# A recommendation tower on one Trainium2 core: a fourth product chunk split in high and low, and the fp32 chunks summed first

## The chip, the core and the metric

The program runs on one core of one Trainium2 chip. The core has five engines with an instruction queue each: PE (TensorE, matrix products), DVE (VectorE), ACT (ScalarE), POOL (GpSimd) and SP (which here only starts transfers). They run side by side and wait for one another through semaphores. The metric is the device time of one execution in microseconds. Three runs of the kernel before gave 1343.85, 1344.63 and 1345.17 us, so its median is 1344.63 us.

## The reference

For each of 1024 samples, 39 embeddings of 16 numbers are looked up. Then comes a "compressed interaction network" of three layers, and then a small dense network:

```
x0 = embeddings                     # [b, 39, 16]
xk = x0
for W in (f0, f1, f2):              # 39*39 x 128, then 128*39 x 128 twice
    z   = einsum('bfd,bgd->bfgd', x0, xk).reshape(b, f*g, d)
    cur = einsum('bpd,pm->bmd', z, W)
    outs.append(cur); xk = cur
result = concat(outs).sum(-1)       # [b, 384]
h = relu([result, dense_ctx] @ W_top1 + b_top1)
h = relu(h @ W_top2 + b_top2)
y = h @ W_top3
```

Layer 1 multiplies pairs of the 39 embeddings. Its products are the operand that this change is about.

## The kernel before

The 1024 samples are 8 batches of 128 samples. A batch is 4 groups, a group is 512 columns (32 samples by 16 numbers), and a group is 4 tiles of 128 columns. So there are 32 groups and 128 tiles; the loop counter `u` counts the 16 tiles of a batch, and `tile` is `u % 4`.

Layer 1 is computed one group ahead. It uses the symmetry of the pairs, which leaves seven chunks of up to 117 product rows. For each group and chunk, DVE forms a 117x512 product (`multiply`, L765, seven per group, at the tiles and banks of `PRODUCTS`), and PE sums the seven into one bank of PSUM (`cin1`, L462). A chunk is summed in one of two ways. Either it goes in as plain fp32, which on PE is one call and two instructions in the trace. Or it is split: ACT rounds the product to a shorter format (`split_high`, L644), POOL subtracts that from the product (`split_low`, L231), and PE makes three short passes (high by high, low weights by high, high weights by low). `SPLIT` names the split chunks: 0, 1 and 2 of seven. The first group of all is summed in fp32 throughout, so 31 groups have split chunks. `HIGHS` says after which tile and bank ACT makes each high part, `POOL_LOWS` in which tile POOL makes each low part, `CIN1` at which tile and bank PE sums a chunk, and `CIN1_ORDER` in which order the chunks come.

Layer 2 is done tile by tile. `cin2` (L482) makes ten banks of 512 columns per tile (the last is 384), each by three passes, into a ring of five banks in PSUM. Four of the ten banks are scaled by ACT (`scale`, L654), the other six are multiplied and added up by DVE (`mac`, L785, 23 instructions per tile). POOL then adds the 16 partial terms of the tile in a tree (`add_up`, L402: three additions at L415 and the last at L419, which writes `x2`). `terms` is double: ACT may start on tile `u` only when POOL has written `x2` of tile `u-2` (the wait at L657), and DVE starts on tile `u` only after ACT's first bank of it (L789).

Layer 3 is summed from `x2` (`sum_s3`, L505; once a batch `cin3`, L516, 78 instructions on PE, which stand between the last three banks of tile 1 of the next batch). POOL also issues the lookups: ten gathers per group (`gather`, L384), three groups ahead, and none for groups 1 to 3 of the last batch. At tile 4 of each of the first seven batches it numbers the rows for the gathers of the next batch (`number_rows`, L381).

The queues are in order and written out by hand. In each tile POOL first makes its low parts, then waits for ACT's and DVE's terms, adds them, and then issues its gathers.

Of the kernel before, what the change touches and what calls it, by code (L numbers as in the profile page):

```python
# [61 lines left out]
TERMS = NA * FB  # L62
W1_CHUNKS = 3
S3_BANK, X1_BANK, MISC_BANK = 5, 6, 7
SPLIT = (0, 1, 2)
NS = len(SPLIT)
CIN1_ORDER = (0, 1, 3, 4, 5, 6, 2)

FIRST_AT, FIRST_BANK = (0, 0), 4
PRODUCTS = ((0, 1), (0, 3), (0, 5), (0, 7), (0, 9), (1, 1), (1, 3))  # L70
SCALARS = (1, 0)
S3_AT = 5
HIGHS = ((0, 2), (0, 4), (0, 7))
POOL_LOWS = {0: (0, 1), 1: (2,)}
CIN1 = ((1, 8), (2, 1), (2, 4), (2, 6), (2, 8), (3, 1), (3, 4))
STORE_X1, SPLIT_X1 = (3, 4), (3, 5)
CIN3 = (7, 8, 9)
# [36 lines left out]
def cin_tower(nc, dense_ctx, ids, first_row, tables, w_top1, b_top1, w_top2, b_top2, w_top3,  # L114
              w0_pair, w0_mirror, f1, f2, c_mask, c_eye, rows, out):
    with ExitStack() as ctx:
# [107 lines left out]

        POOL_PARTS = [i for parts in POOL_LOWS.values() for i in parts]

        def low_ready(gf, i):

            return s_plow, (gf - 1) * len(POOL_PARTS) + POOL_PARTS.index(i) + 1

        def split_low(eng, gf, i):  # L231

            eng.wait_ge(s_high, (gf - 1) * NS + i + 1)
            eng.tensor_tensor(prods_low[:, i, :], prods[0:KR, SPLIT[i], :],  # L234
                              prods_high[:, i, :].bitcast(F32), ALU.subtract).then_inc(low_ready(gf, i)[0], 1)
# [142 lines left out]
        def _(pool):  # L378
# [23 lines left out]
            def add_up(bt, u, front=True):  # L402

                gf = bt * GROUPS + u // TILES + 1
                if front:
                    for i in POOL_LOWS.get(u % TILES, ()):
                        split_low(pool, gf, i)
# [41 lines left out]
        def _(pe):  # L449
# [12 lines left out]
            def cin1(gf, k, first=False):  # L462

                order = range(KT) if first else CIN1_ORDER
                if k == order[0] and not first:
                    pe.wait_ge(s_prod, (gf + 1) * KT)
                if k in SPLIT and not first:
                    i = SPLIT.index(k)
                    pe.wait_ge(*low_ready(gf, i))
                    passes = ((w0_high[:, i, :], prods_high[:, i, :]), (w0_low[:, i, :], prods_high[:, i, :]),  # L470
                              (w0_high[:, i, :], prods_low[:, i, :]))
                else:
                    if first:
                        pe.wait_ge(s_prod, k + 1)
                    passes = ((w0[:, k, :], prods[0:KR, k, :]),)
                for n, (w, x) in enumerate(passes):
                    mm = nc.tensor.matmul(ps[:, X1_BANK, :], w, x, start=(k == order[0] and n == 0),  # L477
                                          stop=(k == order[-1] and n == len(passes) - 1))
                if k == order[-1]:
                    mm.then_inc(s_x1, 1)  # L480
# [66 lines left out]
            def step(bt, u, last):  # L547
# [3 lines left out]
                for q in range(BANKS):  # L551
# [8 lines left out]
                    if front and (tile, q) in CIN1:  # L560
                        n = CIN1.index((tile, q))
                        cin1(gf, CIN1_ORDER[n])
                    if u == 1 and q == BANKS - 1:
# [54 lines left out]
        def _(act):  # L618
# [8 lines left out]
            def store_scalars(gf, j, guard):  # L627
                act.wait_ge(s_st, gf + 1)
                if guard:
                    act.wait_ge(s_mac, gf * (TILES * MACS) - TILES * MACS + CREDIT_MAC)  # L630
                    if j > 1:
                        act.wait_ge(s_s3, gf * TILES - 2 * TILES + 1 + CREDIT_S3)
                nc.scalar.activation(x0_scal[:, j % 2, :, :],
                                     ps[:, MISC_BANK, 0:TILES * F].rearrange("p (t f) -> p t f", f=F),
                                     ACT.Copy).then_inc(s_scal, 1)
# [8 lines left out]
            def split_high(gf, i):  # L644

                act.wait_ge(s_prod, gf * KT + SPLIT[i] + 1)
                nc.scalar.activation(prods_high[:, i, :], prods[0:KR, SPLIT[i], :], ACT.Copy).then_inc(s_high, 1)  # L647

# [61 lines left out]
            def step(bt, u, last):  # L710
# [3 lines left out]
                for q in range(BANKS):  # L714
# [6 lines left out]
                    if front and (tile, q) == SCALARS:  # L721
                        store_scalars(gf, j, True)
                    if front and (tile, q) in HIGHS:
                        split_high(gf, HIGHS.index((tile, q)))
                    if front and (tile, q) == STORE_X1:
# [157 lines left out]
```

## Time and profile before

| | |
|---|---|
| median of three runs | 1344.63 us |
| profiled execution, its own time | 1347.66 us |
| its span, first to last instruction | 1345.8 us |
| mean granted TensorE clock | 0.995 of full |
| PE busy (matmul / weight load) | 95% / 71% |
| POOL busy | 78% |
| DVE busy | 72% |
| ACT busy | 54% |
| chain that ended last | PE 69%, DVE 12%, issue 8%, POOL 6% |

The busy share of PE is that of pipelined matmuls whose ends are modelled, so 95% does not say that PE is what everything waits for. The chain follows one releaser at each step, the one that came last by the records; where two ended almost together, only one is named. So the time of each engine has to be read tile by tile.

### The profile page before, as it was taken

Reading aid. Unit: us, or ns where it says so; the run is one execution under the profiler, and the core shown is the slowest. Engines: PE = TensorE matmul, PEld = TensorE weight load, DVE = VectorE, ACT = ScalarE, POOL = GpSimd, SP = SyncE. Lnnn points to the kernel's source line nnn. Section 1 sums busy time; section 2 is a strip of 40 time slices with the busy share of each in tenths; the row PEclk is TensorE's granted clock in tenths of the full one; section 3 lists DMA queues with packets and bytes.
Section 4 is the critical chain, followed back from the end, with each engine's and each line's share of the span. In section 5 each row is a group of like instructions: output and inputs, shape, how many; then the busy total and the mean of one; then the engine's idle time right before and its main releaser. Section 6 shows DMA issues by size and latency. Waiting matters only on the chain.

```text
span 1345.8 us, 25222 instructions
## 1 busy us (share of the span) xinstructions
PE 1282.5 (95%) x5501; PEld 953.6 (71%) x5501; DVE 968.3 (72%) x3241; ACT 727.6 (54%) x2404; POOL 1052.5 (78%) x937
## 2 busy tenths in 40 slices
PE   0799999999999999999999999999999999999999
PEld 0467778777787777777777776877777777777854
DVE  2657886887757887777768887587877777688820
ACT  2345664566545565555646565465656555466621
POOL 7658888688877988688877888788986898786520
PEclk9989999999999999999999999999999999999999
DMA  5642212222212222122212222112221222121000
GB/s 129 170 120 66 52 44 60 57 56 62 65 35 53 65 64 59 53 65 65 56 33 63 52 64 62 48 47 57 65 61 53 62 65 65 22 65 46 1 0 1
DMA packets 119621, 78.23 MB, mean 58 GB/s; under 512 B 75325, under 2 KB 87715, under 8 KB 119509
## 3 DMA queue, kind: packets, MB, share of 16 engines
q1 hardware_dynamic: 106476, 74.11, 19.5%
q0 software_dynamic: 10240, 2.64, 2.5%
q10 hardware_dynamic: 2792, 0.47, 0.2%
q14 instruction: 101, 0.82, 0.2%
q8 instruction: 12, 0.20, 0.1%
HBM read 18.30 MB, written 2.63 MB: 16 GB/s over the span
## 4 chain that ended last, share of the span: by engine, by line
PE 69%; DVE 12%; issue 8%; POOL 6%; DMA 2%; ACT 1%; SPq 1%; DVEq 1%; ACTq 0%; POOLq 0%
PE ps L498 16%; PE ps L502 15%; PE ps L499 15%; PE ps L477 12%; DVE terms L801 9%; PE ps L522 5%; PE ps L512 3%; DVE prods L773 3%; POOL x_in L387 3%; POOL terms L415 3%; PE ps L578 2%; ACT terms L663 1%; PE ps L588 1%; DMA w<-in_f 1%; POOL prods_low L234 0%
## 5 line engine op out<-in xcount | busy, mean ns | idle before, releaser
L801 DVE SCALAR_TENSOR_TENSOR terms<-ps,x_scal,terms 128x128 f32<-128x128 f32 x2944 | 803.4, 341 | 287.0 <-ACT terms L663 169.8
L663 ACT ACTIVATE terms<-ps,x_scal 128x128 f32<-128x128 f32 x2048 | 584.1, 376 | 417.1 <-PE ps L502 281.7
L415 POOL TENSOR_TENSOR terms<-terms 128x1024 f32<-128x1024 f32 (+2 forms) x384 | 565.8, 1473 | 110.2 <-DVE terms L801 89.3
L498 PE MATMUL ps<-w_high,x_high 128*128 128x512 f32 (+1 forms) x1280 | 591.0, 462 | 28.5 <-DVE terms L801 16.8
L502 PE MATMUL ps<-w_high,x_low 128*128 128x512 f32 (+1 forms) x1280 | 498.4, 389 | 0.0
L499 PE MATMUL ps<-w_low,x_high 128*128 128x512 f32 (+1 forms) x1280 | 496.8, 388 | 0.0
L387 POOL DMA_INDIRECT x_in<-in_tables,row_at x320 | 309.6, 968 | 89.7 <-issue 70.0
L498 PEld LDWEIGHTS ps<-w_high,x_high 128*128 128x128 f32 x1280 | 241.2, 188 | 158.4 <-DVE terms L801 65.5
L499 PEld LDWEIGHTS ps<-w_low,x_high 128*128 128x128 f32 x1280 | 242.3, 189 | 67.3 <-issue 28.1
L502 PEld LDWEIGHTS ps<-w_high,x_low 128*128 128x128 f32 x1280 | 241.1, 188 | 49.7
L477 PE MATMUL ps<-prods,w 117*128 117x512 f32 x262 | 134.9, 600 | 5.0 <-DVE prods L773 5.0
L773 DVE TENSOR_TENSOR prods<-prods,ps 117x512 f32<-117x512 f32 x192 | 129.4, 675 | 2.5 <-DMA prods<-x_cols 2.5
L234 POOL TENSOR_TENSOR prods_low<-prods,prods_high 117x512 fp32r<-117x512 f32 x93 | 118.5, 1290 | 6.7 <-ACT prods_high L647 3.9
L512 PE MATMUL ps<-x_diag,x 128*128 128x320 f32 x256 | 89.7, 432 | 0.0
L647 ACT ACTIVATE prods_high<-prods 117x512 fp32r<-117x512 f32 x93 | 60.6, 652 | 42.0 <-DVE prods L773 42.0
L522 PEld LDWEIGHTS ps<-s,w 128*128 128x128 f32 x624 | 73.0, 192 | 1.7 <-issue 0.5
L419 POOL TENSOR_TENSOR x<-terms 128x128 f32<-128x128 f32 x128 | 58.8, 460 | 19.0 <-POOL terms L415 17.8
L522 PE MATMUL ps<-s,w 128*128 128x128 f32 x624 | 73.2, 275 | 0.0
L477 PEld LDWEIGHTS ps<-prods,w 117*128 117x128 f32 x262 | 50.3, 192 | 19.5 <-issue 7.6
L675 ACT ACTIVATE s<-ps 128x320 f32<-128x320 f32 x128 | 58.1, 454 | 0.6 <-PE ps L512 0.6
L512 PEld LDWEIGHTS ps<-x_diag,x 128*128 128x128 f32 x256 | 48.2, 188 | 11.1 <-issue 0.5
L684 ACT ACTIVATE r<-ps 128x128 f32 (+1 forms) x8 | 2.2, 278 | 73.4 <-PE ps L522 73.4
(42 smaller groups left out, 406.9 us busy)
## 6 DMA issues: line engine op xcount, KB each, us to landing
prods<-x_cols SPq DMA_DIRECT2D x192, 234.0 KB
x_first<-x_cols SPq DMA_DIRECT2D x96, 78.0 KB
x_cols<-x_rows SPq DMA_DIRECT2D x93, 78.0 KB
x_in<-in_tables,row_at POOLq DMA_INDIRECT x320
x_diag<-x_scal SPq DMA_DIRECT2D x256, 9.8 KB
s<-in_f SPq DMA_DIRECT2D x3, 832.0 KB, 9.8
x_rows<-x_in SPq DMA_DIRECT2D x31, 80.0 KB
wt<-in_W_top SPq DMA_DIRECT2D x1, 768.0 KB
```

The source lines that it names most:

```text
L234: eng.tensor_tensor(prods_low[:, i, :], prods[0:KR, SPLIT[i], :], prods_high[:, i, :].bitcast(F32), ALU.subtract).then_inc(low_ready(gf, i ...
L387: pool.indirect_dma_start(out=x0_in[:, j % 2, n, :], out_offset=None, in_=tables, in_offset=bass.IndirectOffsetOnAxis(ap=row_at[:, at:at + ...
L415: nc.gpsimd.tensor_tensor(t[:, 0:n], t[:, 0:n], t[:, n:2 * n], ALU.add).then_inc(s_tree, 1)
L477: mm = nc.tensor.matmul(ps[:, X1_BANK, :], w, x, start=(k == order[0] and n == 0), stop=(k == order[-1] and n == len(passes) - 1))
L498: nc.tensor.matmul(y, x1_high[:, par, at:at + P], high, start=True, stop=False)
L499: nc.tensor.matmul(y, x1_high[:, par, at:at + P], low, start=False, stop=False)
L502: nc.tensor.matmul(y, x1_low[:, par, at:at + P], high, start=False, stop=True) \
L512: nc.tensor.matmul(ps[:, S3_BANK, 0:TB * FX], x2[:, u % 2, :], x0_diag[:, j % 2, t].rearrange("p b f -> p (b f)"), start=True, stop=True). ...
L522: mm = nc.tensor.matmul(ps[:, MISC_BANK, 0:BATCH], w2[:, f, :], s3[:, f, :], start=(f == 0), stop=(f == F - 1))
L663: op = nc.scalar.activation(terms[:, u % 2, FB * ACT_BANKS.index(q) + i, :], ps[:, (BANKS * u + q) % RING, i * G:(i + 1) * G], ACT.Copy, s ...
L773: nc.vector.tensor_tensor(prods[0:KR, k, :], second, ps[0:KR, bank, :], ALU.mult) \
L801: nc.vector.scalar_tensor_tensor(out=acc, in0=y, scalar=x0, in1=acc, op0=ALU.mult, op1=ALU.add).then_inc(s_mac, 1)
```

## The change

A fourth chunk, number 3, is split as chunks 0 to 2 are. ACT makes its high part after bank 9 of tile 0, POOL its low part in tile 1 right behind that of chunk 2, and PE sums it in three short passes instead of one fp32 call. The order in which PE sums the chunks becomes the three fp32 ones (4, 5, 6) and then the four split ones. The prologue splits one more weight chunk (117x128) on ACT and DVE. Nothing else is changed.

```diff
-SPLIT = (0, 1, 2)
+SPLIT = (0, 1, 2, 3)
 NS = len(SPLIT)
-CIN1_ORDER = (0, 1, 3, 4, 5, 6, 2)
+CIN1_ORDER = (4, 5, 6, 0, 1, 2, 3)
 
 FIRST_AT, FIRST_BANK = (0, 0), 4
 PRODUCTS = ((0, 1), (0, 3), (0, 5), (0, 7), (0, 9), (1, 1), (1, 3))
 SCALARS = (1, 0)
 S3_AT = 5
-HIGHS = ((0, 2), (0, 4), (0, 7))
-POOL_LOWS = {0: (0, 1), 1: (2,)}
+HIGHS = ((0, 2), (0, 4), (0, 7), (0, 9))
+POOL_LOWS = {0: (0, 1), 1: (2, 3)}
 CIN1 = ((1, 8), (2, 1), (2, 4), (2, 6), (2, 8), (3, 1), (3, 4))
```

## Rows read from the trace of the kernel before

**Rows 1.** The page, part 1: busy us, share of the span, instructions

```profile
PE 1282.5 (95%) x5501; PEld 953.6 (71%) x5501; DVE 968.3 (72%) x3241; ACT 727.6 (54%) x2404; POOL 1052.5 (78%) x937
```

**Rows 2.** POOL in order of time, one group: start us, us; [idle before <-releaser]

```profile
609.52 2.54 POOL L234 TENSOR_TENSOR prods_low<-prods,prods_high 117x512 fp32r<-117x512 f32 x2
612.00 4.61 POOL L415 TENSOR_TENSOR terms<-terms 128x1024 f32<-128x1024 f32 x3
616.77 0.46 POOL L419 TENSOR_TENSOR x<-terms 128x128 f32<-128x128 f32 x1 [0.16 <-POOL terms L415]
617.43 0.96 POOL L387 DMA_INDIRECT x_in<-in_tables,row_at  x1 [0.20 <-issue]
...
619.66 1.29 POOL L234 TENSOR_TENSOR prods_low<-prods,prods_high 117x512 fp32r<-117x512 f32 x1
620.90 4.56 POOL L415 TENSOR_TENSOR terms<-terms 128x1024 f32<-128x1024 f32 x3
...
646.33 2.53 POOL L234 TENSOR_TENSOR prods_low<-prods,prods_high 117x512 fp32r<-117x512 f32 x2
```

**Rows 3.** The four engines where tile 0 of a batch begins

```profile
204.09 0.46 POOL L419 TENSOR_TENSOR x<-terms 128x128 f32<-128x128 f32 x1 [0.16 <-POOL terms L415]
...
203.55 0.39 PE L502 MATMUL ps<-w_high,x_low 128*128 128x512 f32 x1
...
204.67 1.15 ACT L663 ACTIVATE terms<-ps,x_scal 128x128 f32<-128x128 f32 x4 [1.46 <-PE ps L502]
...
205.94 1.12 DVE L801 SCALAR_TENSOR_TENSOR terms<-ps,x_scal,terms 128x128 f32<-128x128 f32 x4 [0.82 <-ACT terms L663]
```

**Rows 4.** POOL in order of time, the first group of the next batch

```profile
227.45 4.55 POOL L415 TENSOR_TENSOR terms<-terms 128x1024 f32<-128x1024 f32 x3 [0.21 <-DVE terms L801]
...
240.90 4.57 POOL L415 TENSOR_TENSOR terms<-terms 128x1024 f32<-128x1024 f32 x3 [4.62 <-DVE terms L801]
...
250.36 4.59 POOL L415 TENSOR_TENSOR terms<-terms 128x1024 f32<-128x1024 f32 x3 [1.86 <-DVE terms L801]
...
260.74 0.27 POOL L382 TENSOR_TENSOR row_at<-ids_now,ids_base 128x40 uint32<-128x40 uint32 x1 [1.52 <-DMA x_in<-in_tables,row_at]
```

**Rows 5.** What waited for POOL's numbering, 100 to 1250 us: us in total, times, longest

```profile
POOL prods_low L234 <- POOL row_at L382: 1.8, 7, 0.3
```

**Rows 6.** DVE: first product of groups, in mid kernel and in the last batch

```profile
600.64 0.68 DVE L773 TENSOR_TENSOR prods<-x_cols,ps 117x512 f32<-117x512 f32 x1
...
637.41 0.67 DVE L773 TENSOR_TENSOR prods<-x_cols,ps 117x512 f32<-117x512 f32 x1
...
1187.70 0.68 DVE L773 TENSOR_TENSOR prods<-x_cols,ps 117x512 f32<-117x512 f32 x1
...
1223.75 0.68 DVE L773 TENSOR_TENSOR prods<-x_cols,ps 117x512 f32<-117x512 f32 x1
```

**Rows 7.** POOL in the last batch, a group without gathers

```profile
1212.89 4.58 POOL L415 TENSOR_TENSOR terms<-terms 128x1024 f32<-128x1024 f32 x3 [4.01 <-DVE terms L801]
```

**Rows 8.** The chain in order of time, 205 to 265 us: start us, us

```profile
222.25 0.70 PE ps L477 x3
...
233.41 0.86 PE ps L477 x2
```

**Rows 9.** ACT and DVE at the end of tile 0

```profile
256.93 0.69 ACT L647 ACTIVATE prods_high<-prods 117x512 fp32r<-117x512 f32 x1
257.45 1.21 ACT L663 ACTIVATE terms<-ps,x_scal 128x128 f32<-128x128 f32 x4
...
256.63 0.68 DVE L773 TENSOR_TENSOR prods<-prods,ps 117x512 f32<-117x512 f32 x1
...
259.63 1.11 DVE L801 SCALAR_TENSOR_TENSOR terms<-ps,x_scal,terms 128x128 f32<-128x128 f32 x4
```

**Rows 10.** PE at bank 8 of tile 2, and at chunk 2 (tile 3, bank 4)

```profile
623.24 1.02 PE L477 MATMUL ps<-prods,w 117*128 117x512 f32 x2
...
628.95 0.40 PE L477 MATMUL ps<-prods_high,w_high 117*128 117x512 f32 x1
```

**Rows 11.** All chunks of layer 1 on POOL: op xcount, ns min/median/max

```profile
L234 POOL TENSOR_TENSOR prods_low<-prods,prods_high x93: 1268/1291/1313, 51.2 to 1236.3; 117x512 fp32r<-117x512 f32 x93
```

## The prediction, made before the change was built

> **What bounds the kernel now.** The busy shares come first, and they mislead. PE is 95% busy by pipelined matmuls, POOL 78% [rows 1]. On that, and on the chain of waits, which is mostly PE, a cheaper chunk on PE should pay. So I read the engines in order of time, POOL before the others, because the change gives it work.
>
> In the middle of the kernel POOL never waits for another engine. In the group that begins at 609.52 its low parts, trees and gathers stand back to back until the same low parts of the next group at 646.33. What idle time there is, is the 0.16 to 0.30 us between its own instructions [rows 2]. It takes 36.81 us for a group, and a group takes 36.77 us by DVE's first products (600.64 to 637.41) [rows 6]. An engine that waits for nobody, and whose round is the round of the whole, is the bound.
>
> It must also be seen how others wait for it. POOL's `x2` of the third tile of a group ends at 204.55, and ACT starts the tile after the next at 204.67, though PE's last pass for it began at 203.55 and lasted 0.39, so it ended at 203.94. The row puts ACT's idle time down to PE; the last to come was POOL, 0.6 us later. DVE then idles 0.82 us for ACT, and runs on from there [rows 3]. So POOL gates ACT, ACT gates DVE, and DVE frees the banks for PE.
>
> How far is POOL above the next bound? The last batch shows it. There the gathers are gone and POOL waits for DVE again, 4.01 us in one tile [rows 7]. The round of such a group is 36.05 us (1187.70 to 1223.75) [rows 6]. That is PE and DVE by themselves. POOL is the bound by 36.77 - 36.05 = 0.7 us a group and no more, and it stays so only where it gathers.
>
> POOL is not the bound everywhere. In the first group of a batch PE has layer 3 of the batch before as well, and there POOL waits for DVE three times: 0.21, 4.62 and 1.86 us [rows 4]. After the last of them (250.36) it waits for no engine again, only 1.52 us for the landing of its own gathers, up to the first group of the next batch. So a batch is one long POOL run, from the tree of its tile 3 to the `x2` of its tile 14, and then a bridge of PE and DVE of about 46 us (204.55 to 250.28, where DVE ends the terms of tile 3). POOL numbers rows once in each such run, and there are seven of them [rows 5]. The last batch has no such run, for want of gathers.
>
> **The change part by part.** *POOL's fourth low part.* It stands in tile 1 of 31 groups, right behind the low part of chunk 2, in order before the tree. One such instruction lasts 1.27 to 1.31 us [rows 11]. As a second of a pair it adds less: two take 2.54 us together and the tree starts 2.48 us after the first began; a single one has its tree start 1.24 us behind it [rows 2]. I take 1.24 us; the upper end is 1.29. Where does it count? A POOL run holds tile 1 of groups 1, 2 and 3 of a batch (tiles 5, 9 and 13), all before the `x2` of tile 14 where the path leaves POOL. Seven runs with three each are 21 instructions: 21 x 1.24 = 26.0 us (27.1 with 1.29). Nothing hides them, because POOL has no wait in the run that could shrink. The seven others in groups 0 of batches 1 to 7 stand ahead of the tree at 227.45 and of the wait of 4.62 us [rows 4]: that wait becomes about 3.6 us, cost 0. Group 0 of batch 0 is alike, and the two of the last batch stand where POOL has about 4 us to spare [rows 7]: cost 0.
>
> The Trainium skill, page "GPSIMD Engine Reference", section "Elementwise — side-by-side cycle accounting", has about 2.6 cycles per element for a two-input operation, and its Quick Reference has 1.2 GHz: an estimate of 1.11 us for 512 elements, by which the sum would be 21 x 1.11 = 23 us. The row has 1.24 to 1.29 us for this form, so the row is used.
>
> *PE's chunk 3.* An fp32 chunk takes 0.86 us on PE's path and a split one 0.70 us [rows 8]: 0.16 us less in each of 31 groups, 5.0 us in all. In the 21 groups under a POOL run this buys nothing; PE is ahead and waits a little more. On the seven bridges and in two groups of the last batch it counts: 9 x 0.16 = 1.4 us less. The first group of batch 0 starts on a slow clock and puts a long chunk where a short one was; both effects are a few tenths, and I set it at 0.
>
> *The new order.* The first chunk still waits for all seven products, as before, so there is no new wait on PE. The split chunks now come at banks 6 and 8 of tile 2 and at banks 1 and 4 of tile 3. In the group of rows 2, low parts 0 and 1 are done by 612.06; PE stood at bank 8 of tile 2, where part 1 now goes, at 623.24, and at bank 6 some 2 us before. Low part 2 is done at 620.95 and low part 3 would be at about 622.2; PE stood at the last of the chunks, where part 3 now goes, at 628.95, and at the place of part 2 some 3 us before [rows 2, 10]. The margin is 5 us and more, the cost 0. Were it gone, PE would wait in tile 3 with layer 2 queued behind it.
>
> *ACT's fourth high part.* It is placed between bank 7 of tile 0 and bank 0 of tile 1, and needs product 3, which DVE ends at 257.31 where ACT would reach it at 257.45. It delays ACT's bank 0 of tile 1 by the 0.52 us from one start to the next (256.93 to 257.45), from an end at 258.66 to about 259.2; DVE wants that bank at 259.63 [rows 9]. So it is hidden with 0.4 us to spare. Were it not, it would count only in the ten tiles 0 that are not under POOL: at most 10 x 0.52 = 5.2 us. I take 0. DVE gets nothing but one small instruction in the prologue, and ACT likewise, both while POOL issues the first gathers: 0. No transfer is added. POOL's gathers go out 1.24 us later in a group, but they are fetched three groups ahead, and SP's transfers wait for them with some 30 us in hand.
>
> *Sum.* 26.0 - 1.4 = +24.6 us. The profiled execution would go from 1347.66 to 1372.3 us. It lay 3.0 us above the median of its runs, so I forecast 1344.63 + 24.6 = 1369.2 us, 1.8% slower.
>
> **The rivals.** *PE is the bound after all (faster).* Its place is every group, its price the 0.16 us of a chunk, and it decides where POOL has slack of more than 1.24 us per group. Then 31 x 0.16 = 5.0 us would be gained: 1339.6 us. For it speaks PE's 95% and the chain; against it POOL without a wait over 110 us and ACT's start 0.12 us after POOL's `x2` [rows 2, 3]. The Trainium skill, page "Perfetto Trace Analysis", section "Identifying the Most-Contended Engine", says to judge TensorE by the share of weight loads rather than of matmuls; by that it is 71% against POOL's 78%, on the side of the forecast. Chance 4%.
>
> *POOL's cost is taken up in part.* If ACT, DVE and PE, which are delayed with POOL, give POOL shorter waits between instructions, or if a part of a run was bound by PE within its 0.7 us, one in three of the 21 might be hidden: 26.0 x 2/3 - 1.4 = 15.9, or 1360.5 us. Against it: there are no waits in the run to shorten. Chance 5%.
>
> *The low part of group 0 counts too.* POOL comes into tile 1 of group 0 with a wait of only 0.21 us, so a later `x2` of that tile could gate ACT two tiles on, and the path would stay on POOL. Then 28 instructions count: 28 x 1.24 - 1.4 = 33.3, or 1377.9 us. Against it is the wait of 4.62 us in the next tile, on DVE [rows 4]. Chance 5%.
>
> *ACT's high part shows.* Up to 5.2 us on top, 1374.4 us. Chance 6%.
>
> *It does nothing*, because the two effects cancel or the chunk is not split as said: 1344.6 us. Chance 2%.
>
> **How the numbers follow.** The forecast has what is left, 78%. Its own range is 1365.5 (three instructions fewer on the path than I count) to 1372 (1.29 us each and one more). The time named is the forecast's, 1369.2 us. For 8 in 10 I take 1364 to 1375, which holds the forecast and most of the case with ACT. A measurement of this kernel can tell about 0.2% (2.7 us) from no change. Faster by more than that is 0.04, within it 0.03, slower 0.93.
>
> **What the profile after would show.** POOL's low parts should be 124 instead of 93, its busy time up by some 40 us, and its round in mid kernel 38.0 us, still without a wait. The four waits at a batch's start should be there with the one of 4.62 us at about 3.6. The round in the last batch should be 35.9 us. ACT should start tile 4 of a group 0.1 us after POOL's `x2`, with more idle time before it. PE should show new idle time in tiles 0 and 3 of the groups under POOL. The prediction is wrong if POOL shows waits for DVE within a run, if its round stays at 36.8 us, or if PE waits for a low part or DVE for ACT at bank 0 of tile 1.

## The result: 1368.4 us, 1.8% slower, and the profile after

The changed kernel takes 1368.4 us (median of six runs, 1367.85 to 1369.31) against 1344.13 us of the kernel before in the same sessions: +24.3 us, ratio 1.0181, 95% interval 1.0168 to 1.0194. The forecast was +24.6 us and 1369.2 us.

The page after, parts 1 and 4 (busy time; the chain that ended last):

```profile
PE 1287.5 (94%) x5532; PEld 954.5 (70%) x5532; DVE 966.4 (71%) x3242; ACT 740.2 (54%) x2436; POOL 1088.1 (80%) x968
...
POOL 49%; PE 24%; issue 12%; DVE 5%; ACT 5%; DMA 2%; POOLq 1%; SPq 1%; ACTq 0%; DVEq 0%
```

Busy shares hardly moved from [rows 1]; PE still looks like the fullest engine. The chain tells more: POOL's share went from 6% to 49% of the span, PE's from 69% to 24%. Before, many of POOL's releases were put down to PE (in [rows 3] PE had come 0.6 us earlier than POOL). After, ACT's wait for PE fell from 281.7 to 194.0 us in total and that for POOL's `x2` rose from 132.4 to 225.2 us. POOL's own busy time rose by 35.6 us, not by the 40 forecast.

POOL in order of time, one group under a POOL run, and the start of the next (the counterpart of [rows 2]):

```profile
299.32 2.52 POOL L234 TENSOR_TENSOR prods_low<-prods,prods_high 117x512 fp32r<-117x512 f32 x2
301.80 4.55 POOL L415 TENSOR_TENSOR terms<-terms 128x1024 f32<-128x1024 f32 x3
...
309.41 2.54 POOL L234 TENSOR_TENSOR prods_low<-prods,prods_high 117x512 fp32r<-117x512 f32 x2
311.90 4.58 POOL L415 TENSOR_TENSOR terms<-terms 128x1024 f32<-128x1024 f32 x3
...
337.37 2.53 POOL L234 TENSOR_TENSOR prods_low<-prods,prods_high 117x512 fp32r<-117x512 f32 x2
```

The tree of tile 1 now starts 2.49 us behind the low parts where it was 1.24, and the round is 337.37 - 299.32 = 38.05 us instead of 36.81. Still no wait for another engine.

POOL in the first group of a batch (the counterpart of [rows 4]):

```profile
226.21 2.50 POOL L234 TENSOR_TENSOR prods_low<-prods,prods_high 117x512 fp32r<-117x512 f32 x2
228.68 4.55 POOL L415 TENSOR_TENSOR terms<-terms 128x1024 f32<-128x1024 f32 x3
...
241.22 4.58 POOL L415 TENSOR_TENSOR terms<-terms 128x1024 f32<-128x1024 f32 x3 [3.71 <-DVE terms L801]
...
250.45 4.58 POOL L415 TENSOR_TENSOR terms<-terms 128x1024 f32<-128x1024 f32 x3 [1.61 <-DVE terms L801]
```

The wait of 0.21 us is gone, that of 4.62 has become 3.71 and that of 1.86 has become 1.61: the low part of group 0 went into them.

ACT at tile 0 of a group, behind POOL's `x2` (the counterpart of [rows 3]); then DVE's first product of groups in the last batch (of [rows 6]):

```profile
287.55 0.46 POOL L419 TENSOR_TENSOR x<-terms 128x128 f32<-128x128 f32 x1 [0.16 <-POOL terms L415]
...
288.12 1.14 ACT L663 ACTIVATE terms<-ps,x_scal 128x128 f32<-128x128 f32 x4 [3.25 <-POOL x L419]
...
1208.91 0.68 DVE L773 TENSOR_TENSOR prods<-x_cols,ps 117x512 f32<-117x512 f32 x1
...
1244.82 0.68 DVE L773 TENSOR_TENSOR prods<-x_cols,ps 117x512 f32<-117x512 f32 x1
```

ACT starts 0.11 us after POOL's `x2` as before, but idles 3.25 us for it, and the record now names POOL. In the last batch, without gathers, the round is 35.91 us instead of 36.05.

One sign came only in half. PE's new idle time was forecast in tiles 0 and 3 of the groups under POOL. From PE's first bank of a tile to that of the next, tile 0 of the third group takes 9.75 us instead of 8.40 (median of five batches), but the tile 3 before it 8.83 instead of 8.87: nearly all of it lies in tile 0.

**Where the time went, by stretch.** I cut each execution at the starts of POOL's `x2` (L419). A *run* is from tile 3 of a batch to tile 14, a *bridge* from there to tile 3 of the next batch; there are seven of each. The table has the median of the seven, and the last batch from its tile 3 to its last `x2`; what follows that takes 53.8 us in every kernel (us).

| kernel | run | bridge | last batch |
|---|---|---|---|
| before | 104.70 | 51.00 | 101.12 |
| changed | 108.44 | 50.78 | 100.80 |
| e1 new order alone | 104.63 | 51.00 | 101.06 |
| e2 POOL's piece, operand read twice | 107.66 | 50.99 | 101.11 |
| e3 three pieces in group 0 | 104.67 | 50.99 | 101.08 |
| e4 ACT's piece alone | 104.66 | 50.98 | 101.11 |
| e8 POOL's piece, two operands | 108.44 | 50.99 | 101.11 |
| e5 low part 3 on DVE | 105.62 | 50.93 | 100.77 |
| e12 DVE's piece alone | 105.63 | 50.92 | 101.12 |
| e6 low parts 2 and 3 on DVE | 103.18 | 50.86 | 100.78 |
| e7 two chunks split | 100.98 | 52.73 | 101.47 |
| e10 three split, one low part on DVE, early | 102.08 | 51.35 | 101.11 |
| e9 the same, late | 104.84 | 54.21 | 101.39 |
| e11 four split, two on DVE, late | 107.54 | 57.00 | 104.50 |

For the change: 7 x 3.74 = 26.18 us on the runs, 7 x -0.22 = -1.54 on the bridges, -0.32 in the last batch, together +24.3 us, as measured. In every kernel but e9 and e11 one run of the seven, that of the fifth batch, is 1.4 to 1.8 us longer than the median, and the others mostly agree within 0.3 us. In e9 the runs spread over 1.6 us and the bridges over 2.8, in e11 over 3.2 and 4.8, so their medians are rough.

### The profile page after: what moved, and what is told of

Read it like the earlier page. It is cut to its first block, busy times and chain, and to the rows that moved or that the text cites. A ratio compares the mean times of both kernels' runs of the same rounds, so it can differ in the third digit from the quotient of the medians.

```text
span 1366.7 us, 25429 instructions
## 1 busy us (share of the span) xinstructions
PE 1287.5 (94%) x5532; PEld 954.5 (70%) x5532; DVE 966.4 (71%) x3242; ACT 740.2 (54%) x2436; POOL 1088.1 (80%) x968
## 4 chain that ended last, share of the span: by engine, by line
POOL 49%; PE 24%; issue 12%; DVE 5%; ACT 5%; DMA 2%; POOLq 1%; SPq 1%; ACTq 0%; DVEq 0%
POOL terms L415 28%; POOL x_in L387 11%; POOL prods_low L234 7%; PE ps L522 5%; ACT terms L663 5%; DVE terms L801 4%; PE ps L498 4%; PE ps L502 4%; PE ps L499 4%; PE ps L477 3%; POOL x L419 3%; PE ps L578 2%; PE ps L588 1%; DVE prods L773 1%; DMA w<-in_f 1%
## 5 line engine op out<-in xcount | busy, mean ns | idle before, releaser
L663 ACT ACTIVATE terms<-ps,x_scal 128x128 f32<-128x128 f32 x2048 | 582.3, 379 | 431.2 <-POOL x L419 225.2
L498 PE MATMUL ps<-w_high,x_high 128*128 128x512 f32 (+1 forms) x1280 | 582.2, 455 | 48.1 <-DVE terms L801 28.7
L234 POOL TENSOR_TENSOR prods_low<-prods,prods_high 117x512 fp32r<-117x512 f32 x124 | 156.8, 1288 | 6.5 <-ACT prods_high L647 3.6
L477 PE MATMUL ps<-prods,w 117*128 117x512 f32 x200 | 104.0, 607 | 5.0 <-DVE prods L773 5.0
L647 ACT ACTIVATE prods_high<-prods 117x512 fp32r<-117x512 f32 x124 | 76.8, 661 | 42.1 <-DVE prods L773 42.1
L419 POOL TENSOR_TENSOR x<-terms 128x128 f32<-128x128 f32 x128 | 58.7, 459 | 19.0 <-POOL terms L415 17.8
L477 PEld LDWEIGHTS ps<-prods,w 117*128 117x128 f32 x200 | 38.8, 194 | 17.1 <-issue 7.2
L477 PE MATMUL ps<-prods_high,w_low 117*128 117x512 f32 x124 | 49.1, 396 | 0.0
```

Of the source, the lines that this page charges most:

```text
L498: nc.tensor.matmul(y, x1_high[:, par, at:at + P], high, start=True, stop=False)
L663: op = nc.scalar.activation(terms[:, u % 2, FB * ACT_BANKS.index(q) + i, :], ps[:, (BANKS * u + q) % RING, i * G:(i + 1) * G], ACT.Copy, s ...
```

## Experiments

The kernel before took 1343.5 us in the session of e1 to e4, 1342.8 in that of e5 to e7, 1343.8 in that of e8 to e11 and 1343.6 beside e12.

**e1: the order alone.**

```diff
-CIN1_ORDER = (0, 1, 3, 4, 5, 6, 2)
+CIN1_ORDER = (3, 4, 5, 6, 0, 1, 2)
```

> The kernel before with three split chunks, but all fp32 chunks (3, 4, 5, 6) summed first and the split ones (0, 1, 2) behind them: the new order alone. Theory (POOL is the bound, the order costs nothing): 1344 us, within 2 us of the kernel before, and POOL's round stays 36.8 us. Rival (the order makes PE or X1 late, or spares a wait for the low parts): a shift of 3 us or more, with PE or DVE waiting at another place.

Measured: 1342.8 us, ratio 0.9994 (0.9985 to 1.0002). No stretch of the table moves by 0.1 us. The new order is worth nothing that can be told here.

**e2: POOL's piece alone.** Added in tile 1 of every group, behind the low parts:

```diff
+                    if u % TILES == 1:
+                        spare = w0[:, 0:4, :].rearrange("r k m -> r (k m)")
+                        for i in range(1):
+                            pool.tensor_tensor(scratch[:, i, :], spare, spare, ALU.subtract)
```

> The kernel before with one more subtraction of 117x512 on POOL in tile 1 of every group, on constant data into a spare tile; PE, ACT and DVE do what they did. Theory: 21 of them stand in POOL's runs, 21 x 1.24 = 26.0 us, so 1370.1 us (the two of groups 2 and 3 of the last batch and those of groups 0 cost nothing); it should be about 1.4 us above the changed kernel, which has PE's saving too. Rival (PE is the bound and POOL has slack): 1344 us. Rival (group 0 counts as well): 28 x 1.24 = 34.7, 1378.8 us.

Measured: 1364.8 us, ratio 1.0151 (1.0138 to 1.0164). That is 21.3 us, neither 26 nor 35, and 3.0 us less than the change cost (each against the kernel before of its own session), instead of 1.4 more. The place was right (the run is longer by 2.96 us, the bridge and the last batch are as before) and the price was not, as POOL in tile 1 shows:

```profile
271.56 1.29 POOL L235 TENSOR_TENSOR prods_low<-prods,prods_high 117x512 fp32r<-117x512 f32 x1
272.80 1.04 POOL L412 TENSOR_TENSOR scratch<-w 117x512 fp32r<-117x512 f32 x1
273.80 4.55 POOL L420 TENSOR_TENSOR terms<-terms 128x1024 f32<-128x1024 f32 x3
```

The piece adds 1.00 us (272.80 to 273.80), and 21 x 1.00 = 21 us. It read the same columns as both operands; e8 reads two.

**e8: the same with two operands.**

```diff
-                        spare = w0[:, 0:4, :].rearrange("r k m -> r (k m)")
-                            pool.tensor_tensor(scratch[:, i, :], spare, spare, ALU.subtract)
+                        spare = [w0[:, k:k + 4, :].rearrange("r k m -> r (k m)") for k in (0, 3)]
+                        pool.tensor_tensor(scratch[:, 0, :], spare[0], spare[1], ALU.subtract)
```

> As e2_pool_only (the kernel before with one more subtraction on POOL in tile 1 of every group), but the two operands are different columns, where e2 read one operand twice and its instruction took 1.04 us instead of 1.29. Theory: it lasts 1.29 us and adds 1.24 us on POOL, 21 x 1.24 = 26.0 us, about 1369.5 us, 1.5 us above the changed kernel by the same kernel before. Rival (the length of the instruction is not what e2 lacked; the change costs something else besides POOL's time): as e2, 1365 us.

Measured: 1370.2 us, ratio 1.0194 (1.018 to 1.0208), +26.4 us. POOL in tile 1:

```profile
276.50 1.29 POOL L411 TENSOR_TENSOR scratch<-w 117x512 fp32r<-117x512 f32 x1
277.74 4.55 POOL L419 TENSOR_TENSOR terms<-terms 128x1024 f32<-128x1024 f32 x3
```

1.29 us long, 1.24 us on POOL's path, 21 of them: 26.0 us. Its run, 108.44 us, is that of the changed kernel. POOL's fourth low part alone is the whole loss.

**e3: only in group 0.** The piece of e2, three times, with `if u == 1`.

> The kernel before with three more subtractions of 117x512 on POOL, but only in tile 1 of group 0 of each batch (3.7 us there, on constant data into a spare tile). Theory: they fill POOL's waits of 0.21 and 4.62 us in that group and cost nothing: 1344 us, and the wait of 4.62 us becomes about 1.1 us. Rival (the low part of group 0 counts): 7 x 3.7 = 26 us, 1370 us.

Measured: 1344.6 us, ratio 1.0004 (0.9995 to 1.0013). POOL:

```profile
224.40 3.03 POOL L412 TENSOR_TENSOR scratch<-w 117x512 fp32r<-117x512 f32 x3
...
238.10 4.57 POOL L420 TENSOR_TENSOR terms<-terms 128x1024 f32<-128x1024 f32 x3 [1.87 <-DVE terms L807]
```

The pieces have e2's price, 3.0 us together instead of 3.7, so the wait fell to 1.87 and not to 1.1 us. All 3.0 us were hidden in it and in the wait of 0.21 us before it. The rival by which group 0 counts would have given 7 x 3.0 = 21 us; it falls.

**e4: ACT's piece alone.**

```diff
+                    if front and (tile, q) == (0, 9):
+                        act.wait_ge(s_prod, gf * KT + 4)
+                        nc.scalar.activation(scratch[:, 0, :], w0[:, 0:4, :].rearrange("r k m -> r (k m)"), ACT.Copy)
```

> The kernel before with one more ACT copy of 117x512 behind bank 9 of tile 0 of every group, on constant data into a spare tile, with the wait for product 3 that the change has; PE and POOL do what they did. Theory: hidden, with 0.4 us to spare before DVE wants ACT's bank 0 of tile 1: 1344 us. Rival (it shows in the ten tiles 0 that are not under POOL): up to 10 x 0.52 = 5.2 us, 1349 us.

Measured: 1343.4 us, ratio 0.9997 (0.9988 to 1.0005): hidden. ACT and DVE in tile 0, outside a run:

```profile
254.11 0.69 ACT L728 ACTIVATE scratch<-w 117x512 fp32r<-117x512 f32 x1
254.63 1.20 ACT L664 ACTIVATE terms<-ps,x_scal 128x128 f32<-128x128 f32 x4
...
256.30 1.11 DVE L805 SCALAR_TENSOR_TENSOR terms<-ps,x_scal,terms 128x128 f32<-128x128 f32 x4
```

ACT's bank 0 of tile 1 ends at 255.83 and DVE comes for it at 256.30: 0.5 us to spare, where 0.4 had been worked out.

**e7: two chunks split.** The step the other way.

```diff
-SPLIT = (0, 1, 2)
+SPLIT = (0, 1)
-CIN1_ORDER = (0, 1, 3, 4, 5, 6, 2)
+CIN1_ORDER = (0, 1, 2, 3, 4, 5, 6)
-HIGHS = ((0, 2), (0, 4), (0, 7))
-POOL_LOWS = {0: (0, 1), 1: (2,)}
+HIGHS = ((0, 2), (0, 4))
+POOL_LOWS = {0: (0, 1)}
```

> The kernel before with only two chunks split (0 and 1), the step the other way: POOL has 31 low parts less, PE 31 fp32 chunks more. Theory: POOL's round would be 35.5 us, under that of PE and DVE, which becomes 36.05 + 0.16 = 36.2 us; 21 x (36.77 - 36.2) = 12 us are won and 9 x 0.16 = 1.4 us lost: about 1333.7 us. Rival (PE is the bound): 31 x 0.16 = 5 us slower, 1349 us. Rival (POOL is far above all others): 26.0 us won, 1319.5 us.

Measured: 1329.3 us, ratio 0.9897 (0.9883 to 0.9912), 13.5 us faster, though PE has 31 dearer chunks. (ACT has 31 high parts fewer too, whose cost was hidden in e4.) That is neither PE bound (slower) nor POOL far above the rest (24 faster). The table shows how the gain ends: the run is shorter by 3.72 us, three whole low parts, but the bridge is longer by 1.73. POOL's lag behind DVE, 4.5 us at the first tree of a run, is used up along the run. Behind the run POOL waits, at tile 15 (first row) and at tile 1 of the next group 0 (second row), where [rows 4] had 0.21 us:

```profile
660.85 4.60 POOL L415 TENSOR_TENSOR terms<-terms 128x1024 f32<-128x1024 f32 x3 [0.42 <-issue]
...
682.55 4.54 POOL L415 TENSOR_TENSOR terms<-terms 128x1024 f32<-128x1024 f32 x3 [2.73 <-DVE terms L801]
```

So the next group 0 begins where PE and DVE are and not where POOL is. Run and bridge together fell from 155.70 to 153.71, 2.0 us; I had expected 1.5, since I had put POOL 0.7 us a group above PE and DVE. Over three groups that margin is 2.0 plus what PE's dearer chunks take (4 x 0.16), that is about 0.9 us a group.

**e5: low part 3 on DVE.** The changed kernel with

```diff
-POOL_LOWS = {0: (0, 1), 1: (2, 3)}
+POOL_LOWS = {0: (0, 1), 1: (2,)}
+DVE_LOWS = {(2, 6): 3}
```

> The changed kernel with low part 3 made by DVE behind bank 6 of tile 2 instead of by POOL; POOL has its old three. Theory: POOL's round is 36.8 us again and only PE's saving outside POOL's runs is left, 9 x 0.16 = 1.4 us: 1342.7 us. DVE's 0.6 us is hidden, since DVE waits for PE in tile 2. Rival (PE is the bound): 31 x 0.16 = 5.0 us less, 1339 us. Rival (DVE's piece shows in the bridges and the last batch): 9 x 0.6 = 5.4 us, 1348 us.

Measured: 1349.1 us, ratio 1.0046 (1.0033 to 1.0059). My theory missed: POOL had its old three low parts and its run was still 0.92 us longer than before. The last rival has nearly the number but not the place, since the loss is in the runs and not in the bridges. Where DVE is in tile 2 and POOL still at the tree of tile 1, they stood like this:

```profile
619.45 4.95 POOL L421 TENSOR_TENSOR terms<-terms 128x1024 f32<-128x1024 f32 x3
...
621.30 1.12 DVE L240 TENSOR_TENSOR prods_low<-prods,prods_high 117x512 fp32r<-117x512 f32 x1
```

POOL's tree took 4.95 us instead of 4.56 [rows 2], DVE's subtraction 1.12 instead of about 0.68. e12 asks whether that is cause and effect.

**e12: DVE's piece alone**, in the kernel before:

```diff
+                    if front and (tile, q) == (2, 6):
+                        spare = [w0[:, k:k + 4, :].rearrange("r k m -> r (k m)") for k in (0, 3)]
+                        nc.vector.tensor_tensor(scratch[:, 0, :], spare[0], spare[1], ALU.subtract)
```

> The kernel before with one more subtraction of 117x512 on DVE behind bank 6 of tile 2 of every group, from two operands in SBUF into a spare tile, on constant data; nobody waits for it, and POOL, PE and ACT do what they did. Theory (a DVE operation that reads two operands from SBUF holds up POOL's operation beside it, which is what e5 lost): POOL's tree of tile 1 is about 0.3 to 0.4 us longer in the runs, 21 x 0.31 = 6.5 us, about 1350 us, though DVE has idle time in tile 2. Rival (what e5 lost was in the changed kernel's other edits): 1343.8 us, with POOL's instructions as long as before.

Measured: 1350.2 us, ratio 1.0049 (1.0036 to 1.0062), +6.7 us. The run is e5's. Nobody waits for the piece and DVE waits for PE behind it, yet POOL's tree beside it is long again (the first row; the second is a tree of the next tile, without the piece):

```profile
307.11 4.92 POOL L416 TENSOR_TENSOR terms<-terms 128x1024 f32<-128x1024 f32 x3
...
316.32 4.59 POOL L416 TENSOR_TENSOR terms<-terms 128x1024 f32<-128x1024 f32 x3
...
308.96 1.10 DVE L842 TENSOR_TENSOR scratch<-w 117x512 fp32r<-117x512 f32 x1
...
314.01 1.13 DVE L802 SCALAR_TENSOR_TENSOR terms<-ps,x_scal,terms 128x128 f32<-128x128 f32 x4 [1.95 <-PE ps L503]
```

The 21 trees beside the piece take 5.07 us from their start to that of `x2`, the other 107 take 4.74 (medians): 21 x 0.33 = 6.9 us. So a DVE operation with two operands in SBUF holds up POOL, and POOL is what the kernel waits for.

**e6: low parts 2 and 3 on DVE.** As e5, with `POOL_LOWS = {0: (0, 1)}` and `DVE_LOWS = {(2, 4): 2, (2, 8): 3}`.

> The changed kernel with low parts 2 and 3 made by DVE, behind banks 4 and 8 of tile 2; POOL has only 0 and 1. Theory: POOL's round falls to 36.8 - 1.24 = 35.5 us, under that of PE and DVE, which the last batch of the changed kernel shows at 35.9 us. So 21 x (36.77 - 35.9) = 18 us are won, and 1.4 us on PE outside: about 1325 us, and POOL waits for DVE in every group. Rival (DVE's two pieces of 0.6 us show in every group): 31 x 1.2 = 37 us less the gain, some 1360 us.

Measured: 1330.2 us, ratio 0.9915 (0.9895 to 0.9935): 12.6 us faster, two thirds of what the theory had. The run of 103.18 us is 1.5 us shorter than before and not 2.6, and the missing (3.72 - 1.52) / 3 = 0.73 us a group fits two pieces on DVE that hold POOL up by 0.3 to 0.4 us each, as e12 showed for one; no run took the two apart.

**e9 and e10: three chunks split, low part 2 on DVE**, fp32 chunks first, `POOL_LOWS = {0: (0, 1)}`; in e9 `DVE_LOWS = {(3, 1): 2}`, in e10 `{(2, 6): 2}`.

> Three chunks split, fp32 chunks first, low parts 0 and 1 on POOL and low part 2 on DVE behind bank 1 of tile 3, where POOL mostly issues gathers. Against e7_two_split (1329.3 us) PE has 31 x 0.16 us less and POOL the same. Theory (with two low parts on POOL, PE and DVE are the bound; DVE's two-operand subtraction stretches POOL's instruction beside it by at most 0.2 to 0.4 us, which POOL then has to spare): 31 x 0.16 = 5 us less, about 1324.5 us. Rival (DVE's 0.7 to 1.1 us show): 1335 us or more.

> As e9_low2_dve_late, but DVE makes low part 2 behind bank 6 of tile 2, beside POOL's tree, where in e5 DVE took 1.12 instead of 0.67 us and POOL's tree 4.95 instead of 4.57 us. Theory: POOL's round becomes 35.6 + 0.35 = 35.9 us, level with PE and DVE, so 1324.5 to 1327 us, not faster than e9; POOL's tree of tile 1 is longer by 0.35 us. Rival (the stretch is not from DVE's operation): as e9, with no longer tree.

Measured: e9 1359.9 us, ratio 1.0117 (1.0101 to 1.0132); e10 1327.9 us, ratio 0.9883 (0.9868 to 0.9899). e10 lies 0.9 us above the upper end of what the theory gave, and cannot be told from e7, whose interval of 0.9883 to 0.9912 overlaps its own; so its gain is that of two low parts on POOL instead of three, and DVE's work adds none that can be seen. e9 missed by 35 us, on the side of its rival and further. DVE, POOL and PE in tile 3 of e9:

```profile
632.56 3.42 DVE L240 TENSOR_TENSOR prods_low<-prods,prods_high 117x512 fp32r<-117x512 f32 x1
...
632.10 0.95 POOL L393 DMA_INDIRECT x_in<-in_tables,row_at  x1 [0.30 <-issue]
633.07 4.88 POOL L421 TENSOR_TENSOR terms<-terms 128x1024 f32<-128x1024 f32 x3
...
636.04 0.50 PE L483 MATMUL ps<-prods_high,w_high 117*128 117x512 f32 x1 [2.37 <-DVE prods_low L240]
```

The same subtraction that takes 0.68 us alone took 3.42. I had placed it beside POOL's gathers, but POOL's first addition of 1024 columns (2.39 us on average) had come too, and DVE ended 0.5 us after that would. PE stood at the last chunk and waited 2.37 us. Here the margin for the low parts, put at 5 us and more for the changed kernel, where PE never waits for one, was gone, and PE's time was lost outright: 22.6 us in 13 waits, of the 32 us between e9 and e10.

A part of the rest is PE's clock. The granted clock is at its upper level, 2.4 GHz, from 77 us to the end of the last `x2` in the kernel before, the changed kernel and e10. In e9 it is at 1.2 GHz in four stretches of 3.4 us (from 161.0, 478.5, 949.5 and 1109.9 us), each just after a subtraction of over 3.4 us on DVE for which PE had stood; after three more of these it stayed up. The four runs with such a stretch took 104.66 to 104.93 us, two without 103.35 and 103.37: 1.5 us each, about 6 us in all. (The third without is the long one of the fifth batch.) What is left, some 3 us, was not traced.

**e11: four split, two late on DVE.** The changed kernel with `DVE_LOWS = {(3, 1): (2, 3)}` and the last two places of `CIN1` at (3, 3) and (3, 4).

> The changed kernel (four chunks split) with low parts 2 and 3 on DVE behind bank 1 of tile 3, and PE's last two chunks at banks 3 and 4 of tile 3. Against e6_lows23_on_dve (1330.2 us) only the place differs. Theory: POOL's tree is stretched no more in tile 2, a group's POOL round falls from 36.2 to about 35.8, and PE has 31 x 0.32 us less than in e7: about 1322 us. Rival (PE waits for the low parts, or DVE's 1.4 us hold up the ring at tile 3): 1330 us or more, with PE idle before L477.

Measured: 1402.7 us, ratio 1.0437 (1.0421 to 1.0454). It was the rival's case, much worse than its number. What waited on PE, by engine and line (us in total, times, longest), first of e11 and then of e9:

```profile
PE ps L483 <- DVE prods_low L240: 57.9, 31, 3.1
...
PE ps L483 <- DVE prods_low L240: 22.6, 13, 2.4
```

In e11 it is every one of the 31 groups, and weight loads waited besides. The granted clock was at 1.2 GHz in nine stretches between 160 and 1160 us, 40.8 us in all, where e6, with the same two low parts on DVE, had none. How the 72 us between e6 and e11 divide was not worked out. What the idea would bring at a place with margin was not tried.

## Why the prediction was right

**The bound.** The step on which all rests is that POOL, at 78% busy, sets the time and PE, at 95%, does not. e8 shows it: 1.24 us more on POOL per group costs 26.4 us, with nothing changed on the other engines. e7 shows it from the other side: PE gets more work, POOL less, and 13.5 us are won. Of the rivals, that PE is the bound falls by both; that a third of POOL's cost is taken up falls by the runs, which grew by all of it.

**The count of 21.** The forecast took three tiles 1 in each of seven runs and nothing elsewhere. The runs grew by 3.74 us, 3 x 1.24 = 3.72, and e3 shows group 0 to be free. In the last batch nothing was lost either: e8 has 101.11 us there against 101.12, and the change gained PE's 0.32.

**The price.** 1.24 us was read from pairs of low parts [rows 2], and the trees of tile 1 start just so much later. The estimate worked out from the cycles per element that the Trainium skill states, page "GPSIMD Engine Reference", section "Elementwise — side-by-side cycle accounting", and from the clock in the skill's Quick Reference, 1.11 us, would have given 23 us where e8 measured 26.4; the row was right.

**PE's saving.** 9 x 0.16 = 1.4 us was forecast, 7 x 0.22 + 0.32 = 1.9 us came. On PE's path, fp32 and split chunk of the changed kernel cost what they did in [rows 8]:

```profile
234.05 0.86 PE ps L477 x2
236.84 0.70 PE ps L477 x3
```

The rest of the bridge's gain, 0.06 us each, I did not trace.

**What was said to be hidden was hidden.** The order (e1) and ACT's high part (e4) cost nothing that can be measured.

**A size that was off: how far POOL is above the rest.** I read 0.7 us a group from the last batch; e7 puts it at about 0.9. For this change it did not matter, since the step went up from the bound. For a step down it decides the gain, and e7 gained 2.9 us more than expected.

**The time of the profiled execution.** I forecast 1372.3 us, its median plus 3.0; it was 1368.5. The 3.0 us were not the kernel's. The starts of the `x2` of the first batch's tile 3, changed kernel first, then the kernel before:

```profile
95.81 0.46 POOL L419 TENSOR_TENSOR x<-terms 128x128 f32<-128x128 f32 x1 [0.16 <-POOL terms L415]
...
99.42 0.46 POOL L419 TENSOR_TENSOR x<-terms 128x128 f32<-128x128 f32 x1 [0.16 <-POOL terms L415]
```

That one execution of the kernel before was 3.6 us later out of the prologue. The two profiled spans alone, 1366.7 and 1345.8 us, would have shown +20.9 us.

## What to carry to other kernels

The engine that sets the time is the one whose own queue has no wait for another engine over a whole round, whatever its busy share; compare its round with that of the kernel, and look in a stretch where its work is lighter for how far the next bound lies below. Work moved from the fullest engine to that one costs what it adds to that queue times the rounds in which it never waits, and nothing in the rounds where its wait is longer than the work. When work is then moved off it, look at what the receiving instruction does to its neighbour and how long its consumer can wait: with one low part on DVE, e10 was 1.2% faster than the kernel before, and the same instruction five banks later 1.2% slower.

## What the runs showed of the hardware

**DVE and POOL hold each other up.** A DVE subtraction of two SBUF operands, 117x512, takes 0.68 us by itself (the shortest in e5, e9 and e10) and 0.9 to 1.2 us in the middle of POOL's tree (e5, e6, e10, e12), and it took up to 3.48 us in e9. Where it met a first or second addition of a tree, it ended 0.54 to 0.56 us behind that addition's end in e5, e9, e10 and e12, and the tree was 0.33 us longer (e12). Beside gathers alone it took 0.68 us in e9 (once 0.72), and the seven gathers that began inside it lasted 1.21 to 1.29 us instead of about 0.95. DVE's operations with one operand in PSUM ran beside the same trees at their usual length: in the kernel before, the products took 0.67 to 0.69 us and the multiply-adds 0.33 to 0.35 from the shortest to the longest.

The Trainium skill, page "SBUF — State Buffer", section "SBUF: two separate sides", says that a DVE operation with two SBUF inputs and a POOL operation that reads SBUF exclude each other for a whole instruction, and that the one that starts first goes first. The trace agrees on the first: in e12 and in e9 DVE came to its end only behind POOL's addition of 2.4 us, and held up the next. On the second it does not by its recorded starts: in the group of e9 that is shown, DVE's record starts 0.51 us before that of POOL's addition, and DVE was still the one to wait. What decides there no run shows.

**A POOL subtraction that reads one operand twice is shorter.** It took 1.04 us with the same columns as both operands (e2) and 1.28 us with two (e8, and 1.29 for the low parts), in the same form of 117x512. A stand-in for an instruction must have its operands too.
